# Four-part transformer block: the five layer normalisations of a group applied on ScalarE instead of VectorE

## What is computed

```python
x = x + L0_xattn(_layernorm(x), ctx)   # one head; inside it both inputs are normalised again with gain and bias
x = x + L0_ffn(_layernorm(x))          # 64 slots: gelu router, top 8, GRU-like update, slot values back to the tokens
x = x + L1_xattn(_layernorm(x), ctx)   # 16 heads of 16, then a 256-512-256 relu network
x = x + L1_ffn(_layernorm(x))          # 8 experts, the best 2 of each token

def _layernorm(x, eps=1e-05):
    return (x - mean(x)) / sqrt(var(x) + eps)
```

## Time and profile before

| | |
|---|---|
| median of 3 runs | 740.45 us (737.38 to 744.55) |
| the profiled execution's own time | 736.18 us |
| its span | 734.3 us |
| mean granted clock of TensorE | 0.937 |
| busy: TensorE, its weight loads | 628.2, 514.6 us |
| busy: VectorE, ScalarE, POOL | 334.3, 222.0, 180.9 us |

### The profile page before, as it was taken

The page is one execution under the profiler, slowest core; times in us unless marked ns, Lnnn a source line. Parts: engine busy times, 40 slices in busy tenths (PEclk is TensorE's granted clock), DMA queues, the critical chain, the costliest instruction groups (busy, mean ns, idle before and its releaser), DMA issues.

```text
span 734.3 us, 11628 instructions
## 1 busy us (share of the span) xinstructions
PE 628.2 (86%) x4286; PEld 514.6 (70%) x4287; DVE 334.3 (46%) x805; ACT 222.0 (30%) x361; POOL 180.9 (25%) x151
## 2 busy tenths in 40 slices
PE   4968689999799998899998799405999999999993
PEld 3747456787467686476876577305999999999993
DVE  4444638736748638468554577482111111111110
ACT  1232045621445431445421542001222222222220
POOL 2100222100412002312002220024444444544522
PEclk9997799999999999899998999656999999999998
DMA  9800100000300002100001000144888888888841
GB/s 349 341 1 21 58 1 1 1 22 2 114 0 0 0 21 71 43 0 0 0 0 57 1 1 1 58 149 135 253 235 252 236 224 250 239 231 244 241 91 21
DMA packets 26378, 72.86 MB, mean 99 GB/s; under 512 B 4496, under 2 KB 18064, under 8 KB 21104
## 3 DMA queue, kind: packets, MB, share of 16 engines
q1 hardware_dynamic: 14352, 57.67, 22.4%
q0 software_dynamic: 7488, 10.39, 8.8%
q10 hardware_dynamic: 4512, 4.46, 1.8%
HBM read 62.87 MB, written 9.64 MB: 99 GB/s over the span
## 4 chain that ended last, share of the span: by engine, by line
PE 70%; issue 10%; DVE 8%; ACT 4%; POOL 3%; DVEq 2%; DMA 1%; POOLq 0%; ACTq 0%
PE ps L618 54%; PE ps L959 9%; PE ps L622 7%; POOL var_xh L307 1%; ACT ring L483 1%; DVE mx L1116 1%; DVEq L1029 1%; DVE ring L1120 1%; POOL ring L364 1%; DVE rc L1126 1%; DVE XH L997 1%; DVE arena L1028 1%; ACT arena L407 1%; ACT L483 1%; DMA arena<-in_x 1%
## 5 line engine op out<-in xcount | busy, mean ns | idle before, releaser
L618 PE MATMUL ps<-keep,arena 128*128 128x128 f32 (+2 forms) x1344 | 165.9, 281 | 0.8 <-ACT arena L432 0.8
L618 PEld LDWEIGHTS ps<-keep,arena 128*128 128x128 f32 x1344 | 159.8, 193 | 5.6 <-ACT arena L432 3.9
L1389 DVE TENSOR_TENSOR keep<-keep,ps 128x512 f32<-128x512 f32 x39 | 26.9, 690 | 175.3 <-PE ps L618 170.8
L378 POOL DMA_INDIRECT out_x<-OT,row_no x39 | 61.7, 1583 | 114.0 <-ACT OT L596 98.0
L307 POOL TENSOR_TENSOR var_xh<-var_xh,minus_half 128x4 f32<-128x4 f32 x16 | 16.9, 1058 | 250.6 <-DVE var_xh L992 250.6
L618 PE MATMUL ps<-arena,keep 128*128 128x256 f32 (+1 forms) x184 | 70.2, 533 | 5.9 <-DVE arena L1056 2.8
L959 PE MATMUL ps<-w2e,keep 128*128 x312 | 73.6, 380 | 0.0
L618 PE MATMUL ps<-ring,V 128*32 128x128 f32 x512 | 64.0, 278 | 1.5 <-DVE OT L1128 1.5
L618 PE MATMUL ps<-ring,keep 128*32 128x128 f32 x512 | 63.5, 273 | 0.0
L1116 DVE TENSOR_REDUCE mx<-ps 128x8 f32<-128x1024 f32 x32 | 39.0, 1220 | 53.5 <-PE ps L618 53.5
L959 PEld LDWEIGHTS ps<-w2e,keep 128*128 128x128 f32 x312 | 56.4, 191 | 6.0
(11 more groups left out here) (201 smaller groups left out, 844.6 us busy)
## 6 DMA issues: line engine op xcount, KB each, us to landing
arena<-in_w SPq DMA_DIRECT2D x39, 1024.0 KB
w2e<-in_w SPq DMA_DIRECT2D x8, 512.0 KB, 22.4
keep<-in_keep SPq DMA_DIRECT2D x1, 3075.0 KB, 20.7
ring<-in_fold SPq DMA_DIRECT2D x1, 2112.0 KB, 12.2
arena<-in_x SPq DMA_DIRECT2D x4, 512.0 KB, 3.6
arena<-in_ctxT SPq DMA_DIRECT2D x4, 512.0 KB, 4.1
out_x<-X ACTq DMA_DIRECT2D x4, 512.0 KB, 3.1
normed<-XH ACTq DMA_DIRECT2D x4, 512.0 KB, 4.0
```

The costliest lines, as they stand in the source:

```text
L378: pool.indirect_dma_start(out=out_d, out_offset=bass.IndirectOffsetOnAxis(ap=row_no[:, t:t + 1], axis=0), in_=YO[t % DEEP], in_offset=None ...
L618: ins = pe.matmul(out, w, m, start=(k == 0), stop=(k == len(pairs) - 1))
L1389: dve.tensor_tensor(HA[r % 2], HA[r % 2], ps[:, 2 * (r % 2) + 1, :], ALU.mult).then_inc(act_ok, 1)
```

## The change

Step 3 moves to ScalarE. VectorE writes minus the mean into a new small tile off ahead of var. POOL's root now signals itself (rt_name), waits for that signal, multiplies off by the root, and only then signals rs_name. ScalarE's norm waits for rs_name and runs four ACTIVATE with the function Identity, root as the scale column and off as the bias column. Each norm is called at the head of the function that copies the transposed block, so rows_turned first normalises, then waits for the transposes, then copies.

```diff
--- before.py
+++ after.py
@@ -159,6 +159,7 @@
         stat = {m: sb(f"stat_{m}", [P, GB, 6]) for m in norms}
         mv = {m: sb(f"mv_{m}", [P, GB, 2]) for m in norms}
         var = {m: sb(f"var_{m}", [P, GB]) for m in norms}
+        off = {m: sb(f"off_{m}", [P, GB]) for m in norms}
         minus_half = sb("minus_half", [P, GB])
         mark = sb("mark", [P, 1])
         nm = sb("nm", [P, GB])
@@ -210,7 +211,7 @@
                  "xh2 xT2_ps xT2 h_ps h lg_ps top ex al aT_ps aT ws_ps si_ps gi gx_ps rz rz_act n_pre n_act sn sv_ps sv fo_ps x2 "
                  "xh3 xb xT3_ps xT3 k_ps k v1_ps v1 q1_ps q1 f_ps f y_ps xh4 xT4_ps xT4 gl_ps gl "
                  "kb sc_ps sub exp pt_ps pt ot_ps ot")
-        names += "".join(f" var_{m} rs_{m}" for m in norms)
+        names += "".join(f" var_{m} rt_{m} rs_{m}" for m in norms)
         s = {n: sem("s_" + n) for n in names.split()}
         fold_ps, fold_ok = sem("fold_ps"), sem("fold_ok")
         v1_zero, half_set = sem("v1_zero"), sem("half_set")
@@ -304,7 +305,9 @@
         def _(pool):
             def root(n, name):
                 pool.wait_ge(s["var_" + name], n + 1)
-                pool.tensor_tensor(var[name][:, :], var[name][:, :], minus_half[:, :], ALU.pow).then_inc(s["rs_" + name], 1)
+                pool.tensor_tensor(var[name][:, :], var[name][:, :], minus_half[:, :], ALU.pow).then_inc(s["rt_" + name], 1)
+                pool.wait_ge(s["rt_" + name], n + 1)
+                pool.tensor_tensor(off[name][:, :], off[name][:, :], var[name][:, :], ALU.mult).then_inc(s["rs_" + name], 1)
 
             def roots_in(m):
                 root(m, "xh")
@@ -392,11 +395,19 @@
         @block.scalar
         def _(act):
 
+            def norm(n, src, out, width, name):
+                act.wait_ge(s["rs_" + name], n + 1)
+                for t in range(GB):
+                    ins = act.activation(out[:, t, 0:width], src[:, t, 0:width], ACT.Identity, bias=off[name][:, t:t + 1], scale=var[name][:, t:t + 1])
+                ins.then_inc(s[name], 1)
+
             def rows_turned(m):
+                norm(m, X0, XH0, D, "xh")
                 act.wait_ge(s["xT_ps"], m + 1)
                 act.copy(xT0, ps[:, 0:2, :]).then_inc(s["xT"], 1)
 
             def context_turned(m):
+                norm(m, C, CH, DC, "ch")
                 act.wait_ge(s["cT_ps"], m + 1)
                 act.copy(CT[:, 0, :], bank(2))
                 act.copy(CT[:, 1, :], bank(7)).then_inc(s["cT"], 1)
@@ -423,6 +434,7 @@
                 act.copy(PT, split(bank(2), GB)).then_inc(s["pT"], 1)
 
             def rows2_turned(m):
+                norm(m, X0, XH0, D, "xh2")
                 act.wait_ge(s["xT2_ps"], m + 1)
                 act.copy(xT0[:, 0, :], bank(2))
                 act.copy(xT0[:, 1, :], bank(0)).then_inc(s["xT2"], 1)
@@ -462,6 +474,7 @@
                 ins.then_inc(s["k"], 1)
 
             def rows3_turned(n):
+                norm(n, X1, XH3, D, "xh3")
                 act.wait_ge(s["xT3_ps"], n + 1)
                 act.copy(xT0, ps[:, 1:3, :]).then_inc(s["xT3"], 1)
 
@@ -495,6 +508,7 @@
                 ins.then_inc(s["f"], 1)
 
             def rows4_turned(n):
+                norm(n, X4, XH4, D, "xh4")
                 act.wait_ge(s["xT4_ps"], n + 1)
                 act.copy(xT1[:, :, :], ps[:, 3:5, :]).then_inc(s["xT4"], 1)
 
@@ -989,24 +1003,16 @@
                 for t in range(GB):
                     dve.bn_aggr(mv[name][:, t, :], stat[name][:, t, :])
                 settle()
+                dve.tensor_scalar(off[name][:, :], mv[name][:, :, 0], -1.0, None, ALU.mult)
                 dve.tensor_scalar(var[name][:, :], mv[name][:, :, 1], scale, eps, ALU.mult, ALU.add).then_inc(s["var_" + name], 1)
-
-            def norm(n, src, out, width, name):
-                dve.wait_ge(s["rs_" + name], n + 1)
-                for t in range(GB):
-                    ins = dve.tensor_scalar(out[:, t, 0:width], src[:, t, 0:width], mv[name][:, t, 0:1], var[name][:, t:t + 1],
-                                            ALU.subtract, ALU.mult)
-                ins.then_inc(s[name], 1)
 
 
             def norm_in(m):
                 dve.wait_ge(x_in, 16 * (m + 1))
 
                 spread_of(X0, D, "xh", 1.0 + EPS, EPS * EPS)
-                norm(m, X0, XH0, D, "xh")
                 dve.wait_ge(c_in, 16 * (m + 1))
                 spread_of(C, DC, "ch")
-                norm(m, C, CH, DC, "ch")
 
             def most(m):
                 dve.wait_ge(s["s_ps"], m + 1)
@@ -1240,7 +1246,6 @@
             folded()
             add_attention(0)
             gather_stats("xh2")
-            norm(0, X0, XH0, D, "xh2")
             top(0)
             shares(0)
             dve.wait_ge(fold_ps, 6)
@@ -1253,7 +1258,6 @@
             slot_values(0)
             add_slots(0)
             gather_stats("xh3")
-            norm(0, X1, XH3, D, "xh3")
             dve.wait_ge(fold_ps, 7)
             dve.tensor_tensor(ab1_col[:, :], ps[:, 7, 0:H1 // P], kept("ab1"), ALU.add)
             with dve.Fori(0, LAST) as n:
@@ -1269,7 +1273,6 @@
                 divide(n, 1)
                 gather_stats("xh2")
                 shift(n, 4)
-                norm(n + 1, X0, XH0, D, "xh2")
                 divide(n, 2)
                 shift(n, 5)
                 divide(n, 3)
@@ -1291,8 +1294,6 @@
                 gather_stats("xh4")
                 add_slots(n + 1)
                 gather_stats("xh3")
-                norm(n, X4, XH4, D, "xh4")
-                norm(n + 1, X1, XH3, D, "xh3")
             for u in range(UNITS):
                 shift(LAST, u, 0 if u % 2 else 3)
                 if u >= 2:
@@ -1303,7 +1304,6 @@
             add_outputs(LAST, 0)
             add_outputs(LAST, 1)
             gather_stats("xh4")
-            norm(LAST, X4, XH4, D, "xh4")
             route(B - GB, B)
 
             dve.wait_ge(counted, 1)
```

## The result

With the change the kernel takes 791.3 us in the median (785.0 to 796.6) against 739.8 in the same comparison, 1.068 times as long (95% interval 1.059 to 1.078): 51.5 us slower. Forecast were 787 us and a range of 764 to 806.

What follows compares the result with a forecast made beforehand. The prediction took a chain through TensorE, whose order is fixed, as the bound. It added 33.9 us for ScalarE's queues and 16.5 for the clock to 736.18, giving 786.6, told as 787 us, with an 80% range of 764 to 806.

Steps and rivals of the forecast that it cites:

- the queues: Norms standing behind other work in ScalarE's program delay TensorE: 4.4 + 14.8 + 9.8 + 4.9 = 33.9 us.
- the clock: TensorE's granted clock falls after the new waits, slowing matmuls: 16.5 us, with 0 and 30 as ends.
- The price of a group: Four 128x256 ACTIVATE with scale and bias columns on ScalarE: 2.01 us, against 1.38 on VectorE.
- The offset's price: POOL's added 128x4 multiply behind each power: 0.15 us, plus 0.05 and 0.05, so each root 0.25 later.
- Place A: rows4 and rows3: XH3's norm queues behind the copy of XH4's result, turn_x3 1.47 us late; 4.4 us in three iterations.
- Place B: rows and context: norms of x and context queue on ScalarE, turn_context 4.46 us late; 14.8 us in all.
- the supplement of 1.4 us for the first: First iteration's turn_context: 1.42 us extra loss on top of 4.46, since ch is ready sooner there.
- Place C: rows2: xh2's norm queues behind the copy of probabilities, turn_x2 3.27 us late; 9.8 us in three iterations.
- Outside the loop: First xh, xh2, xh3 and last xh4 cost 0.9 us each, plus a 1.28 us table load: 4.9 us.
- Removed from VectorE: 20 groups of 1.4 us and more leave VectorE; gain costed at nothing, except where the group ended TensorE's wait.
- The rival of the held clock: Whole kernel: the clock holds despite the new waits, leaving only 33.9 us added: 770 us, chance 0.22.
- The rival of stalls given back: TensorE's later waits shrink or ACTIVATE is at its lower bound; 20 of 33.9 us left: 756 us, chance 0.12.

Runs made afterwards that it cites:

- filled pair: Changed kernel and kernel before, each with matmuls that nobody reads put in TensorE's waits: 759.3 us against 731.1 us.
- hoist: Changed kernel with all five normalisations still on ScalarE, same instructions, only called earlier in its program: 754.0 us, ratio 1.020 to the kernel before.
- before_fill: Kernel before the change, with unread 128x512 matmuls put in TensorE's waits: 731.1 us, ratio 0.989 to the kernel before.
- undo_b: Changed kernel with the xh and ch normalisations back on VectorE: 763.3 us, ratio 1.029 to the kernel before.
- a_only: Kernel before with only the xh3 and xh4 normalisations moved to ScalarE: 745.5 us, ratio 1.007.
- warm: Changed kernel with unread matmuls in TensorE's loop waits around turn_x, turn_context, the attention query and turn_x3, none ahead of turn_x2: 768.8 us, ratio 1.035.
- mixed: Kernel before with only xh (called ahead of query1) and xh4 normalised on ScalarE; ch, xh2 and xh3 stay on VectorE: 736.1 us, ratio 0.995.
- c_only: Kernel before with only the xh2 normalisation moved to ScalarE: 749.5 us, ratio 1.010.
- undone places: Changed kernel with one part back on VectorE at a time: xh2 774.9 us, xh3 and xh4 771.5 us, xh and ch 763.3 us.

## Why the prediction was right, and where it wasn't

The sum was 33.9 us for the queues and 16.5 for the clock, 50.4; measured were 51.5. The filled pair splits the measured one: some 28 us for the queues, and the remaining 23 for the clock. **The total was better than its terms**: one was 6 too high, the other 7 too low, and that they cancelled was luck.

- **The price of a group**, 2.01 us worked out: 2.07 for four and 0.59 for one. Right. The 2.06 us estimated by the Trainium skill ("ScalarE: Activation LUTs", What ACT_TABLE_LOAD costs) are nearer than my line between two lengths.
- **The offset's price**, 0.15 us for the multiply: 0.20. The two small terms beside it, 0.05 each, were taken from no row; in the profile after, the multiply starts 0.07 us behind the root's end (202.68 and 202.61), and VectorE's added instruction puts var some 0.07 us later (off starts at 201.28, var at 201.35). A root is thus some 0.34 us later and not 0.25, hidden in the loop as the prediction had it, but for the 0.28 seen in hoist.
- **Place A**: 3.1 us of wait and 1.47 late. The wait was 3.07, and from TensorE's being ready for XH4 to turn_x3 it is 4.10 us against 2.73, so 1.4 late. Right.
- **Place B**: a wait of 3.4 us at turn_x: 3.31. From turn_x3 to turn_context it is 14.58 us in the third iteration filled, against 10.25 in before_fill: 4.3 late for 4.46. Right. The step that failed is the supplement of 1.4 us for the first: filled, that iteration is 110.2 us long, no longer than the third. The early turn_context of the earlier trace rows stood behind a slow query1. In the kernel before, the context's norm ended 9.7 us after the start of turn_x3 in the first iteration and 10.1 in the second, nearly alike, but turn_x started 9.6 and 6.2 us after it, with query1 at 6.67 us against 3.68. I took for an early norm what was a late turn_x.
- **Place C**: 3.27 us late, three times: waits of 3.07. Right. Alone it cost 8.8 us (7.5 by the ratio) against 10.7 worked out with its part outside the loop, with some clock in it both ways.
- **Outside the loop**, 4.9 us: filled, the two kernels reach turn_x3(0) 2.2 us apart, and what stands behind the loop is 0.9 shorter. Too high by more than 3. Where the rest went, no run shows.
- **Removed from VectorE: nothing.** True for the change as it stands. undo_b and a_only show that the removal of XH4's and XH3's norms is worth 1.35 us at turn_context as soon as ScalarE isn't the later one.
- **The clock**, 16.5 with 30 as the upper end: the net is some 23, the step that was mis-sized. I counted an attention query at the other level for each new low stretch at A and B, 3.0 us, and 1.5 after C. In the changed kernel's trace the clock is low for 10.2 us behind A and again for 13.6 from turn_x on, so turn_x, score1 and turn_context are slow too, each on the path: the third iteration takes 119.4 us against 110.6 filled. After C it didn't fall at all. In the loop the two errors nearly cancel: the change lengthens the profiled loop by 45.1 us unfilled and by 26.5 filled, so 18.6 are clock, against 16.5. The larger part of the miss lies outside the loop, where I put the clock at nothing: 9.6 us unfilled against 1.3 filled, some 8 of clock (these are profiled executions, whose clock parts add up to 26.8 and not to 23).

The rival of the held clock, 770 us, meant the queues' price on top of a clock as before. Its 33.9 us for the queues were too many as well. That warm lands on 768.8 is no test of it: its clock is held in part and still falls behind C. The rival of stalls given back has a grain of truth: TensorE's idle time grew by 26.2 us (106.1 to 132.3), less than 33.9. Slow matmuls can fill such time, but the filled pair, with few of them, also gives 28, so they are not the whole reason.

The Trainium skill ("Perfetto Trace Analysis", Optimizing Scalar/DVE Operations) says that moving work off VectorE may make sense when VectorE is saturated. This case doesn't contradict it: VectorE was busy 46% of the time, and the full move cost 51.5 us. But at the same busy share mixed moves two of the five groups at no cost, and hoist all five for 14, so the busy share didn't decide what the move cost.

## What to carry to other kernels

Ask of a moved step what stands ahead of it in its new engine's program, not how busy that engine is: with the same instructions called earlier, 37 of the 51.5 us were gone. Where a handful of waits of 2 to 4 us appear on TensorE's path, cost the granted clock behind them as a term of its own; here it was nearly as large as the waits, and it doesn't add up place by place. Filling waits with matmuls that nobody reads paid in the change (22.5 us at A and B alone) and in the kernel before (7.5).

## What the runs showed of the hardware

- The same wait of 3.07 us at C was followed at once by a fall of the granted clock in two iterations of c_only (eight transposes in 1.20 and 1.97 us) and one of warm (1.51), not at once in their other iterations (in the third of warm it fell within 10 us), and not in the 14 us behind it in any of the changed kernel (1.09). What decides it was not found.
- Shorter waits were followed by one too: in the third iteration of the kernel before, waits of 0.57, 1.36 and 1.26 us stand ahead of an attention query of 6.69 us instead of 3.67. The same waits in the second iteration were not followed by one.
- The undone places sum to 64.2 us for a change of 51.5. That the clock makes them interact is likely, not shown by itself.
- Four VectorE tensor_scalar of 128x256 that take 1.38 us take 2.09 with a POOL tensor_tensor of 1.04 us beside them (mixed); four ScalarE ACTIVATE of the same shape took 2.06 to 2.08 in the rows shown.
